# Moving the set-up of the TT weights and the transposes of W3 behind the first four layer-norm tiles

## The chip, the cores and the metric

The kernel runs on all 8 cores of one Trainium2 chip, each core taking one batch element. No core talks to another. The time is device microseconds of the slowest core.

## The reference

For each batch element x (4096 rows of 1024 numbers) the reference computes one block:

```python
xn = _layernorm(x, axis=-1)
Q = xn @ W1 + b1;  K = xn @ W2 + b2;  V = xn @ W3 + b3
attn = softmax(einsum('bse,bte->bst', Q, K) / 32)
a = einsum('bst,bte->bse', attn, V) @ W4 + b4
W_real = einsum('abcd,cefg->abefdg', G1_R, G2_R).reshape(512, 512)   # W_imag alike
out_real = xr @ W_real.T - xi @ W_imag.T + bias_real    # xr, xi: halves of xn
out_imag = xr @ W_imag.T + xi @ W_real.T + bias_imag
x = x + a + concatenate([out_real, out_imag], axis=-1)
```

## The kernel before

Every instruction is put on a list by `P.add(engine, ...)`. Each engine runs its own part of this list in exactly that order; a `waits=[...]` entry becomes a semaphore wait in front of the instruction, and everything later on the same engine stands behind it. DMAs issued by SP, ACT and POOL are entries of those engines' lists too.

The program has four stages.

1. **Prologue.** SP issues four loads of the small TT factors (G1 and G2, real and imaginary), then 16 loads of one column each of `b1` and `b2`, 8 of `b3`, and three bias rows. All 31 count on one semaphore; `PRO` is the wait for all of them. POOL issues the cast load of W3 into `Wproj` (line 211) and eight cast loads of W4 (line 215), and then makes the identity matrix `ident` and the ones (lines 218 to 223). DVE casts `b3` (line 226, `b3c`, waits for `PRO`) and permutes G2 (line 229, `g2perm`, waits for `PRO`). `emit_g(0)` does 8 rounds of a float32 matmul (line 236) and a DVE eviction (line 243) through the one PSUM tile `sp_a`, and ends with a 1 MB store to scratch by SP. Then PE transposes W3 in 32 pairs (lines 258 and 261, through `ptA` and `ptB`) and DVE evicts each pair into `W3T` (line 264). POOL's cast load of W2 (line 269, `LW2`) overwrites `Wproj`, so it waits for the last of these transposes.
2. **First tiles and group 0.** A layer-norm tile is 128 rows. `emit_ln_load` issues its 512 KB load on ACT into one of two slots of `xg`; the load of tile t waits until tile t-2 has been normalised. `emit_ln_stats` is four DVE instructions (lines 284 to 294), `emit_ln_apply` two ACT instructions, one DVE instruction (line 309) and one POOL instruction (line 313), and `emit_ln_tps` four pairs of PE transposes, each evicted by DVE (line 337) into `xnT`. Tiles 0 to 3 are done in pairs, ahead of the loop over groups. Group 0 then does both halves of its K projection (`emit_khalf`, line 357, which waits for W2 and for its tiles), and the prologue's tail: `emit_g(1)`, the product of W3 and W4 (line 402), the bias row, and 64 small read-backs of the scratch (line 449) that DVE turns into `Wq2` (line 455). Then come its V projection (line 379) and the next group's tiles. DVE reaches the evictions of tiles 4 and 5 only behind line 455.
3. **Groups 1 to 7** do K, V and the next group's tiles.
4. **Attention** over 32 row tiles, from about 460 us to the end, with the next rows' layer norm and Q projection in between.

The order of PE's list at the start of the program is: the matmuls of `emit_g(0)`, the transposes of W3, the transposes of tiles 0 to 3, K of group 0. DVE's list has `b3c` and `g2perm` first, then the matching evictions, then the statistics of tile 0. POOL's list has W3, W4, `ident`, W2, and then the normalisation of tile 0.

Of the kernel before, what the change touches and what calls it, by code (L numbers as in the profile page):

```python
# [9 lines left out]
ALU = mybir.AluOpType  # L10
# [62 lines left out]
def build_nc(T=4096):  # L73
# [11 lines left out]
    w2_d = nc.dram_tensor("W2", [D, D], F32, kind="ExternalInput").ap()  # L85
# [5 lines left out]
    g1r_d = nc.dram_tensor("G1R", [1, 32, 4, 32], F32, kind="ExternalInput").ap()  # L91
    g2r_d = nc.dram_tensor("G2R", [4, 16, 1, 16], F32, kind="ExternalInput").ap()
    g1i_d = nc.dram_tensor("G1I", [1, 32, 4, 32], F32, kind="ExternalInput").ap()
    g2i_d = nc.dram_tensor("G2I", [4, 16, 1, 16], F32, kind="ExternalInput").ap()
# [3 lines left out]
    scr_d = [nc.dram_tensor(f"scr{ri}", [1024, 256], F32).ap() for ri in range(2)]  # L98
# [7 lines left out]
    Wproj = E(nc.sbuf_tensor("Wproj", [128, 8, D], BF16))  # L106
# [8 lines left out]
    ident = E(nc.sbuf_tensor("ident", [128, 128], BF16))  # L115
# [3 lines left out]
    b3c = E(nc.sbuf_tensor("b3c", [128, 8], BF16))  # L119
    b3f = E(nc.sbuf_tensor("b3f", [128, 8], F32))  # L120
# [15 lines left out]
    ones1 = cbs[0:2, 1024:1152]  # L136
# [3 lines left out]
    if full:  # L140
        W3T = KT[:, :, 2048:3072]
    else:
        W3T = None
# [5 lines left out]
    else:  # L149
# [6 lines left out]
        W3T = W3T_t[:, :, :]  # L156
        pro_flat = pro_t[:, :]

    out2 = pro_flat[:, 0:4096].bitcast(F32).rearrange("p (q n) -> p q n", q=8)
    wqst = [pro_flat[:, 4096 + 1024 * k:4096 + 1024 * (k + 1)].bitcast(F32)  # L160
            for k in range(2)]
# [3 lines left out]
    g1p = pro_flat[0:4, 12288:16384].bitcast(F32).rearrange(  # L165
        "p (ri n) -> p ri n", ri=2)
    g2n = pro_flat[0:4, 16384:17408].bitcast(F32).rearrange(
        "p (ri n) -> p ri n", ri=2)
# [10 lines left out]

    semnames = ["q_sy", "q_t", "q_v", "q_s", "q_g",  # L180
                "d_pro", "d_wg", "d_xg0", "d_xg1", "d_xr", "d_out",
                "d_scw", "d_sra", "d_srb", "d_w10", "d_w11", "d_w12", "d_w13", "d_cbl", "d_wgB"]
    sems = {n: E(nc.semaphore(n)) for n in semnames}

    P = Prog()
# [3 lines left out]
    def proload(key, out_ap, in_ap):  # L189
        P.add("sync", lambda e, o=out_ap, i=in_ap: e.dma_start(o, i),  # L190
              mark=key, dma_sem="d_pro")

    proload(("Lg1r",), g1p[:, 0, :],
            bass.AP(g1r_d.tensor, 0, [[32, 4], [128, 32], [1, 32]]))
    proload(("Lg1i",), g1p[:, 1, :],
            bass.AP(g1i_d.tensor, 0, [[32, 4], [128, 32], [1, 32]]))
    proload(("Lg2r",), g2n[:, 0, :],
            bass.AP(g2r_d.tensor, 0, [[256, 4], [1, 256]]))
    proload(("Lg2i",), g2n[:, 1, :],
            bass.AP(g2i_d.tensor, 0, [[256, 4], [1, 256]]))  # L200
    for c in range(8):
        proload(("Lb1", c), b1s[:, c:c + 1], b1_d[c * 128:(c + 1) * 128].unsqueeze(1))
        proload(("Lb2", c), b2s[:, c:c + 1], b2_d[c * 128:(c + 1) * 128].unsqueeze(1))
    for c in range(8):
# [3 lines left out]
    proload(("Lbi",), cbrow[:, 512:1024], bi_d.unsqueeze(0))  # L208
    PRO = ("Lbi",)

    P.add("gpsimd", lambda e: e.dma_start(
        Wproj[:, :, :], w3_d.rearrange("(c p) n -> p c n", p=128)),
        mark=("LW3",), dma_sem="d_wg")
    for k4 in range(8):
        P.add("gpsimd", lambda e, k4=k4: e.dma_start(
            W4b[:, k4, :], w4_d[128 * k4:128 * (k4 + 1), :]),
            mark=("LW4", k4), dma_sem="d_wgB")
    P.add("gpsimd", lambda e: e.memset(ident[:, :], 0.0), mark=("id1",))
    P.add("gpsimd", lambda e: e.affine_select(
        out=ident[:, :], in_=ident[:, :], compare_op=ALU.not_equal, fill=1.0,  # L220
        base=0, pattern=[[-1, 128]], channel_multiplier=1),
        waits=[("id1",)], mark=("id2",))
    P.add("gpsimd", lambda e: e.memset(ones1, 1.0), mark=("ones",))
    WG0 = ("LW4", 7)

    P.add("vector", lambda e: e.tensor_copy(b3c[:, :], b3f[:, :]),
          waits=[PRO], mark=("Lb3c",))

    P.add("vector", lambda e: e.tensor_copy(
        g2p[:, :, :].rearrange("p ri (g e) -> p ri g e", g=16),  # L230
        g2n[:, :, :].rearrange("p ri (e g) -> p ri g e", e=16)),
        waits=[PRO], mark=("g2perm",))

    def emit_g(ri):
        for q in range(8):
            P.add("tensor", lambda e, ri=ri, q=q: e.matmul(
                sp_a[:, 0:256], g1p[:, ri, q * 128:(q + 1) * 128],
                g2p[:, ri, :], start=True, stop=True),
                waits=[PRO, ("g2perm",), free["sp_a"],
                       ("Gev", ri, q - 1) if q > 0 else  # L240
                       (("Gev", ri - 1, 7) if ri > 0 else None)],
                mark=("Gmm", ri, q))
            P.add("vector", lambda e, ri=ri, q=q: e.tensor_copy(
                out2[:, q, :], sp_a[:, 0:256]),
                waits=[("Gmm", ri, q)] + ([("scw", 0)] if ri == 1 else []),
                mark=("Gev", ri, q))
        P.add("sync", lambda e, ri=ri: e.dma_start(
            scr_d[ri].rearrange("(q p) n -> p q n", p=128), out2[:, :, :]),
            waits=[("Gev", ri, 7)],
            mark=("scw", ri), dma_sem="d_scw")  # L250
        free["sp_a"] = ("Gev", ri, 7)

    emit_g(0)
    for p2 in range(32):
        i, j2 = divmod(p2, 4)
        bank, bk = (ptA, "ptA") if p2 % 2 == 0 else (ptB, "ptB")
        j0 = 2 * j2
        P.add("tensor", lambda e, i=i, j0=j0, bank=bank: e.transpose(
            bank[:, 0, :], Wproj[:, i, j0 * 128:(j0 + 1) * 128], ident[:, :]),
            waits=[("LW3",), ("id2",), free[bk]], mark=None)  # L260
        P.add("tensor", lambda e, i=i, j0=j0, bank=bank: e.transpose(
            bank[:, 1, :], Wproj[:, i, (j0 + 1) * 128:(j0 + 2) * 128], ident[:, :]),
            mark=("w3tp", p2))
        P.add("vector", lambda e, i=i, j0=j0, bank=bank: e.tensor_copy(
            W3T[:, j0:j0 + 2, i * 128:(i + 1) * 128], bank[:, :, :]),
            waits=[("w3tp", p2)], mark=("w3te", p2))
        free[bk] = ("w3te", p2)

    P.add("gpsimd", lambda e: e.dma_start(
        Wproj[:, :, :], w2_d.rearrange("(c p) n -> p c n", p=128)),  # L270
        waits=[("w3tp", 31)], mark=("LW2",), dma_sem="d_wg")

    def emit_ln_load(gt):
        slot = gt % 2
# [49 lines left out]
    def emit_ln_tps(gt, phase, extra_tp):  # L324
        u = gt % 4
        slot = gt % 2
        for p4 in range(4):
            bank, bk = (ptA, "ptA") if p4 % 2 == 0 else (ptB, "ptB")
            c0 = 2 * p4
            xw = [("lnap", gt), free[bk]] + (list(extra_tp) if p4 == 0 else [])  # L330
            P.add("tensor", lambda e, c0=c0, slot=slot, bank=bank: e.transpose(  # L331
                bank[:, 0, :], xnn[:, slot, c0 * 128:(c0 + 1) * 128], ident[:, :]),
                waits=xw + [("id2",)], mark=None)
            P.add("tensor", lambda e, c0=c0, slot=slot, bank=bank: e.transpose(  # L334
                bank[:, 1, :], xnn[:, slot, (c0 + 1) * 128:(c0 + 2) * 128], ident[:, :]),
                mark=("xtp", gt, p4))
            P.add("vector", lambda e, u=u, c0=c0, bank=bank: e.tensor_copy(  # L337
                xnT[:, u, c0:c0 + 2, :], bank[:, :, :]),
                waits=[("xtp", gt, p4)], mark=("xte", gt, p4))
            free[bk] = ("xte", gt, p4)  # L340
        if phase == 2:
            P.add("gpsimd", lambda e, u=u: e.tensor_scalar_mul(
                ngxT[:, u, :],
                xnT[:, u, 4:8, :].rearrange("p c n -> p (c n)"), -1.0),
                waits=[("xte", gt, 2), ("xte", gt, 3)], mark=("ngx", gt))
# [112 lines left out]
        WQDONE = ("Wqcv", 1, 3)  # L458


    for u in range(2):
        emit_ln_load(u)
        emit_ln_stats(u)
# [8 lines left out]
        emit_ln_apply(u)  # L472
    for u in range(2, 4):
        emit_ln_tps(u, 1, [])
    for g in range(NGRP):
        nphase = 2 if g == NGRP - 1 else 1
        for u2 in range(2):
            emit_ln_load(4 * (g + 1) + u2)
            emit_ln_stats(4 * (g + 1) + u2)
        emit_khalf(g, 0)  # L480
        for u2 in range(2):
            emit_ln_apply(4 * (g + 1) + u2)
        if g == 0:
            emit_khalf(g, 1)
            emit_prologue_tail()
        emit_v(g, 0)
        emit_v(g, 1)
        for u2 in range(2):
            emit_ln_tps(4 * (g + 1) + u2, nphase,
                        [("Kmm", 0, g, 7), ("Vmm", g, u2, 1)])  # L490
        for u2 in range(2, 4):
            emit_ln_load(4 * (g + 1) + u2)
            emit_ln_stats(4 * (g + 1) + u2)
        if g > 0:
            emit_khalf(g, 1)
        for u2 in range(2, 4):
            emit_ln_apply(4 * (g + 1) + u2)
        emit_v(g, 2)
        emit_v(g, 3)
        for u2 in range(2, 4):  # L500
            emit_ln_tps(4 * (g + 1) + u2, nphase,
                        [("Kmm", 1, g, 7), ("Vmm", g, u2, 1)])
# [237 lines left out]
```

How the kernel before makes its waits and increments, by code:

```python
            def body(eng):  # L53
                seen = waited[engname]
                for e, fn, rw, mi in self.ops:
                    if e != engname:
                        continue
                    for semname, val in rw:
                        if seen.get(semname, -1) >= val:
                            continue
                        eng.wait_ge(sems[semname], val)
                        seen[semname] = val
                    ins = fn(eng)
                    if mi is not None:
                        semname, val, inc = mi
                        ins.then_inc(sems[semname], inc)
```

## Time and profile before

| | us |
|---|---|
| two timed runs | 1748.47 and 2000.08 |
| their median | 1874.27 |
| the profiled execution | 1748.35 |
| its span on the slowest core | 1746.6 |
| spans of the 8 cores | 1741.6 to 1746.6 |
| PE busy in the span | 1549.8 (89%) |
| DVE busy | 765.8 (44%) |
| ACT busy | 493.1 (28%) |
| POOL busy | 130.9 (7%) |

The span runs from the first to the last instruction of the slowest core, 1.75 us less than the time of that execution. A matmul's row is its time in the pipeline, so the busy time of PE overstates how near it is to its peak. Engines are PE (TensorE), PEld (its weight loads), DVE (VectorE), ACT (ScalarE), POOL (GpSimd) and SP (SyncE); SPq and ACTq are their queues issuing DMAs. PEclk is the granted clock of TensorE, 1.00 being 2.4 GHz.

### The profile page before, as it was taken

Reading aid. Unit: us, or ns where it says so; the run is one execution under the profiler, and the core shown is the slowest. Engines: PE = TensorE matmul, PEld = TensorE weight load, DVE = VectorE, ACT = ScalarE, POOL = GpSimd, SP = SyncE. Lnnn points to the kernel's source line nnn. Section 1 sums busy time; section 2 is a strip of 40 time slices with the busy share of each in tenths; the row PEclk is TensorE's granted clock in tenths of the full one; section 3 lists DMA queues with packets and bytes.
Section 4 is the critical chain, followed back from the end, with each engine's and each line's share of the span. In section 5 each row is a group of like instructions: output and inputs, shape, how many; then the busy total and the mean of one; then the engine's idle time right before and its main releaser. Section 6 shows DMA issues by size and latency. Waiting matters only on the chain.

```text
span 1746.6 us, 25605 instructions; the slowest of 8 cores (1741.6 to 1746.6 us)
## 1 busy us (share of the span) xinstructions
PE 1549.8 (89%) x8496; PEld 762.3 (44%) x8496; DVE 765.8 (44%) x1872; ACT 493.1 (28%) x865; POOL 130.9 (7%) x113
## 2 busy tenths in 40 slices
PE   0477299999899999999999999999999999999998
PEld 0143165655444444444444444444444444444443
DVE  0423233333355535553553555355535544553554
ACT  0010033333233323323223233233232232332322
POOL 1010011111100000000000000000000000000000
PEclk9989599999999999999999999999999999999999
DMA  7411421121411111101110111111111111110001
GB/s 122 93 52 32 43 71 60 63 73 49 136 45 38 37 37 37 45 29 42 45 51 35 41 45 37 37 37 38 36 37 49 49 36 37 49 37 25 25 25 37
DMA packets 69756, 83.49 MB, mean 48 GB/s; under 512 B 39923, under 2 KB 50171, under 8 KB 69630
## 3 DMA queue, kind: packets, MB, share of 16 engines
q1 hardware_dynamic: 57182, 42.02, 8.2%
q10 hardware_dynamic: 9216, 33.56, 5.8%
q0 software_dynamic: 3232, 6.29, 2.2%
q8 instruction: 72, 1.18, 0.3%
q14 instruction: 54, 0.44, 0.1%
HBM read 69.27 MB, written 18.87 MB: 50 GB/s over the span
## 4 chain that ended last, share of the span: by engine, by line
PE 85%; DVE 5%; SPq 4%; issue 3%; DMA 2%; ACT 0%; DVEq 0%; POOL 0%; ACTq 0%; POOLq 0%
PE po L558 13%; PE po L663 12%; PE po L659 12%; PE sp_a L558 6%; PE sp_b L558 6%; PE pf L588 3%; PE sp_a L357 3%; PE sp_b L357 3%; PE po L379 3%; PE pf L379 3%; PE sp_b L525 3%; PE sp_a L525 3%; PE ptA L630 2%; PE ptB L630 2%; DVE QXT L337 2%
## 5 line engine op out<-in xcount | busy, mean ns | idle before, releaser
L663 PE MATMUL po<-V,ETs 128*128 128x512 bf16 x1024 | 388.0, 379 | 0.0
L659 PE MATMUL po<-V,ETs 128*128 128x512 bf16 x1024 | 388.0, 379 | 0.0
L558 PE MATMUL po<-KT,QXT 128*128 128x512 bf16 x1024 | 231.5, 379 | 0.0
L614 ACT ACTIVATE Et<-Ssb,ngm 128x512 bf16<-128x512 f32 x256 | 181.2, 719 | 165.5 <-PE ptB L630 139.0
L618 DVE TENSOR_REDUCE r<-Et 128x1 f32<-128x512 bf16 x256 | 173.7, 679 | 31.1 <-ACT Et L614 31.1
L313 POOL TENSOR_SCALAR xnn<-xg,rstd,nmr 128x1024 bf16<-128x1024 f32 x64 | 76.2, 1196 | 1231.8 <-DVE nmr L309 1217.1
L558 PEld LDWEIGHTS po<-KT,QXT 128*128 128x128 bf16 x1024 | 100.2, 98 | 120.9
L563 DVE TENSOR_REDUCE mx<-po 128x1 f32<-128x512 f32 x128 | 88.6, 692 | 129.6 <-PE po L558 129.6
L663 PEld LDWEIGHTS po<-V,ETs 128*128 128x128 bf16 x1024 | 100.1, 98 | 94.3
L659 PEld LDWEIGHTS po<-V,ETs 128*128 128x128 bf16 x1024 | 100.0, 98 | 94.4
L571 ACT ACTIVATE Ssb<-sp_a 128x512 f32<-128x512 f32 x64 | 38.2, 597 | 341.5 <-DVE mx L563 188.0
L642 DVE COPY ETs<-ptA 128x256 bf16<-128x256 bf16 x256 | 73.5, 287 | 134.4 <-PE ptB L630 98.2
L558 PE MATMUL sp_a<-KT,QXT 128*128 128x512 bf16 x512 | 120.9, 379 | 7.7 <-ACT QXT L533 7.7
L558 PE MATMUL sp_b<-KT,QXT 128*128 128x512 bf16 x512 | 120.9, 379 | 0.0
L571 ACT ACTIVATE Ssb<-po 128x512 f32<-128x512 f32 x128 | 76.4, 597 | 142.0 <-DVE mx L563 142.0
L331 PE MATMUL ptA<-ident,xnn 128*128 128x128 bf16 x128 | 28.3, 221 | 95.8 <-DVE QXT L337 77.0
L337 DVE COPY QXT<-ptA 128x256 bf16<-128x256 bf16 x128 | 37.4, 292 | 156.2 <-PE ptB L334 96.9
L563 DVE TENSOR_REDUCE mx<-sp_a 128x1 f32<-128x512 f32 x64 | 44.1, 689 | 135.7 <-PE sp_a L558 135.7
L630 PE MATMUL ptA<-ident,Et 128*128 128x128 bf16 x512 | 70.4, 219 | 24.9 <-DVE ETs L642 15.2
L692 DVE SCALAR_TENSOR_TENSOR xr<-po,rrv,xr 128x1024 f32<-128x1024 f32 x32 | 41.1, 1284 | 92.1 <-PE po L663 92.1
L558 PEld LDWEIGHTS sp_a<-KT,QXT 128*128 128x128 bf16 x512 | 49.5, 98 | 70.0 <-issue 11.4
L630 PEld LDWEIGHTS ptA<-ident,Et 128*128 128x128 bf16 x512 | 41.5, 97 | 82.7 <-issue 50.6
(95 smaller groups left out, 1809.9 us busy)
## 6 DMA issues: line engine op xcount, KB each, us to landing
xg<-x ACTq DMA_DIRECT2D x64, 512.0 KB, 3.6
xr<-x SPq DMA_DIRECT2D x32, 512.0 KB, 3.5
out<-xr SPq DMA_DIRECT2D x32, 512.0 KB, 2.6
Wproj<-W POOLq DMA_DIRECT2D x2, 2048.0 KB, 21.1
Ssb<-W SPq DMA_DIRECT2D x8, 512.0 KB, 8.0
KT<-W POOLq DMA_DIRECT2D x8, 256.0 KB, 25.9
scr<-V SPq DMA_DIRECT2D x2, 1024.0 KB, 4.5
V<-scr SPq DMA_DIRECT2D x64, 32.0 KB, 2.5
```

The costliest lines, as they stand in the source:

```text
L313: P.add("gpsimd", lambda e, s=s: e.tensor_scalar(xnn[:, s, :], xg[:, s, :], rstd[:, s, 0:1], nmr[:, s, 0:1], ALU.mult, ALU.add), waits=[(" ...
L357: e.matmul(spv[:, off:off + 256], Wproj[:, k, c * 128:(c + 1) * 128], xnT[:, 2 * half:2 * half + 2, k, :], start=(k == 0), stop=(k == 7)),
L379: P.add("tensor", lambda e, u=u, h=h, k=k, pv=pv: e.matmul(pv[:, h * 512:(h + 1) * 512], xnT[:, u, k, :], W3p[:, k, h * 512:(h + 1) * 512] ...
L525: P.add("tensor", lambda e, r=r, k=k, spv=spv: e.matmul(spv[:, :], Wproj[:, r, k * 128:(k + 1) * 128], xnT[:, :, k, :], start=(k == 0), st ...
L558: P.add("tensor", lambda e, tb=tb, c=c, si=si, spv=spv: e.matmul(spv, QT[:, c, si * 128:(si + 1) * 128], KT[:, c, tb * 512:(tb + 1) * 512] ...
L563: P.add("vector", lambda e, tb=tb, spv=spv: e.reduce_max(mx8[:, tb:tb + 1], spv, axis=AX.X), waits=[("Smm", i, tb)], mark=("Smx", i, tb))
L571: P.add("scalar", lambda e, tb=tb, spv=spv: e.activation(Ssb[:, tb * 512:(tb + 1) * 512], spv, AF.Identity), waits=scw_, mark=("Scp", i, tb))
L614: P.add("scalar", lambda e, tb=tb: e.activation(Et[:, tb % 2, :], Ssb[:, tb * 512:(tb + 1) * 512], AF.Exp, bias=ngm[:, 0:1], scale=SCALE), ...
L618: P.add("vector", lambda e, tb=tb: e.reduce_sum(r8[:, tb:tb + 1], Et[:, tb % 2, :], axis=AX.X), waits=[("exp", i, tb)] + ([("rr", i - 1)] ...
L630: e.transpose(bank[:, qq, :], Et[:, tb % 2, q * 128:(q + 1) * 128], ident[:, :]),
L659: P.add("tensor", lambda e, tb=tb, q=q, tj=tj: e.matmul(po[:, 0:512], ETs[:, tb % 2, q, :], V0[:, tj, 0:512], start=(tj == 0), stop=(tj == ...
L663: P.add("tensor", lambda e, tb=tb, q=q, tj=tj: e.matmul(po[:, 512:1024], ETs[:, tb % 2, q, :], V0[:, tj, 512:1024], start=(tj == 0), stop= ...
```

## The change

Five things are changed, and no instruction is added to or taken from the program:

- The four loads of G1 and G2 count on a semaphore of their own, and `GLD` is the wait for them. `PRO` is now the wait for the other 27 loads.
- `ident` and the ones are made by POOL ahead of its loads of W3 and W4.
- `b3c`, with its wait for `PRO`, stands directly ahead of the loop that starts layer-norm tile 0.
- `g2perm` and `emit_g(0)`, which now wait for `GLD` in place of `PRO`, and the 32 pairs of transposes of W3 with their evictions stand behind the layer norm and the transposes of tiles 0 to 3.
- The load of W2 stands behind these, and so behind the normalisation of tiles 0 to 3 in POOL's list.

```diff
+    P.add("gpsimd", lambda e: e.memset(ident[:, :], 0.0), mark=("id1",))
     P.add("gpsimd", lambda e: e.dma_start(
         Wproj[:, :, :], w3_d.rearrange("(c p) n -> p c n", p=128)),
         mark=("LW3",), dma_sem="d_wg")
...
-    P.add("vector", lambda e: e.tensor_copy(b3c[:, :], b3f[:, :]),
-          waits=[PRO], mark=("Lb3c",))
...
+    P.add("vector", lambda e: e.tensor_copy(b3c[:, :], b3f[:, :]),
+          waits=[PRO], mark=("Lb3c",))
+
     for u in range(2):
         emit_ln_load(u)
         emit_ln_stats(u)
...
     for u in range(2, 4):
         emit_ln_tps(u, 1, [])
+    P.add("vector", lambda e: e.tensor_copy(
+        g2p[:, :, :].rearrange("p ri (g e) -> p ri g e", g=16),
+        g2n[:, :, :].rearrange("p ri (e g) -> p ri g e", e=16)),
+        waits=[GLD], mark=("g2perm",))
...
+                waits=[GLD, ("g2perm",), free["sp_a"],
...
+    emit_g(0)
...
+    P.add("gpsimd", lambda e: e.dma_start(
+        Wproj[:, :, :], w2_d.rearrange("(c p) n -> p c n", p=128)),
+        waits=[("w3tp", 31)], mark=("LW2",), dma_sem="d_wg")
+
     for g in range(NGRP):
```

## Rows read from the trace of the kernel before

**Rows 1.** Spans and mean granted TensorE clock, two of eight cores
```profile
core 2: 1746.6 us, clock 0.980
...
core 4: 1746.6 us, clock 0.978
```

**Rows 2.** Stages: length, busy PE PEld DVE ACT POOL, clock, DMA share, GB/s
```profile
0.00:34.60 34.60, 0.00 (x0) 0.00 (x0) 0.00 (x0) 0.00 (x0) 6.18 (x16) 1.00 0.98 153
...
64.90:88.50 23.60, 4.45 (x32) 2.36 (x33) 11.08 (x34) 2.91 (x9) 5.66 (x5) 1.00 0.75 161
...
160.10:203.20 43.10, 0.00 (x0) 0.00 (x0) 3.32 (x8) 0.50 (x1) 0.00 (x0) 0.53 0.59 73
```

**Rows 3.** Chain that ended last, 60 to 92 us: start, length, what
```profile
71.61 9.80 DMA xg<-x
```

**Rows 4.** Timeline of the first 50 us: start, length, engine, line, operation
```profile
1.56 1.06 POOL L211 DMA_DIRECT2D Wproj<-W  x1 [0.87 <-POOLq L79]
...
6.81 0.31 POOL L218 MEMSET ident<- 128x128 bf16 x1
...
7.56 0.19 POOL L223 MEMSET cbs<- 2x128 bf16 x1
...
29.87 0.25 SPq L190 DMA_DIRECT2D V<-bim  x1
...
34.63 0.17 DVE L226 CAST b3c<-b3f 128x8 bf16<-128x8 f32 x1 [34.63 <-DMA V<-bim]
```

**Rows 5.** Timeline from 64 to 89 us, the same columns
```profile
64.70 0.69 DVE L284 BATCH_NORM_STATS2 bn<-xg 128x6 f32<-128x512 f32 x1
...
64.94 0.92 POOL L269 DMA_DIRECT2D Wproj<-W  x1 [57.19 <-PE ptB L261]
...
70.42 1.52 ACTq L278 DMA_DIRECT2D xg<-x  x2
...
74.04 0.29 DVE L337 COPY QXT<-ptB 128x256 bf16<-128x256 bf16 x1
...
81.50 0.69 DVE L284 BATCH_NORM_STATS2 bn<-xg 128x6 f32<-128x512 f32 x1 [0.89 <-DMA xg<-x]
...
88.54 1.91 PE L357 MATMUL sp_a<-QXT,Wproj 128*128 128x256 bf16 x8
...
88.85 0.29 DVE L337 COPY QXT<-ptB 128x256 bf16<-128x256 bf16 x1
```

**Rows 6.** Loads of tile xg from 0 to 110 us, issue to landing
```profile
DMA to landing us min/median/max: 3.5/4.9/9.8
```

**Rows 7.** DMA, 65 to 82 us: packets, MB, share; an issue's landing
```profile
q0 software_dynamic: 1040, 2.10, 73.2%
...
q10 hardware_dynamic: 288, 1.05, 17.8%
...
Wproj<-W POOLq DMA_DIRECT2D x1, 2048.0 KB, 17.0
```

**Rows 8.** Core 2 by line: min/median/max ns, first and last start; W2's landing
```profile
L226 DVE CAST b3c<-b3f x1: 172/172/172, 39.1 to 39.1; 128x8 bf16<-128x8 f32 x1
...
L269 POOL DMA_DIRECT2D Wproj<-W x1: 914/914/914, 69.4 to 69.4; - x1
...
L357 PE MATMUL sp_a<-QXT,Wproj x64: 269/272/418, 94.1 to 108.8; 128*128 128x256 bf16 x64
...
Wproj<-W POOLq DMA_DIRECT2D x1, 2048.0 KB, 19.6
```

**Rows 9.** Timeline: V projection of tiles 2 and 3 of group 0
```profile
206.12 5.91 PE L379 MATMUL po<-Ssb,QXT 128*128 128x512 bf16 x16
...
211.86 3.62 PE L379 MATMUL pf<-Ssb,QXT 128*128 128x512 bf16 x16
```

**Rows 10.** Line 455, cores 2 and 4: duration ns, first and last start
```profile
L455 DVE CAST Wq<-V x8: 426/427/428, 174.0 to 204.0; 128x512 bf16<-128x512 f32 x8
...
L455 DVE CAST Wq<-V x8: 426/427/428, 169.4 to 202.9; 128x512 bf16<-128x512 f32 x8
```

More of the change, by code:

```diff
@@ L181, in build_nc @@
                 "d_pro", "d_wg", "d_xg0", "d_xg1", "d_xr", "d_out",
-                "d_scw", "d_sra", "d_srb", "d_w10", "d_w11", "d_w12", "d_w13", "d_cbl", "d_wgB"]
+                "d_scw", "d_sra", "d_srb", "d_w10", "d_w11", "d_w12", "d_w13", "d_cbl", "d_wgB", "d_gld"]
     sems = {n: E(nc.semaphore(n)) for n in semnames}
@@ L191, in proload, with gload @@
               mark=key, dma_sem="d_pro")
[L193 to L200, printed above, removed]
+    def gload(key, out_ap, in_ap):
+        P.add("sync", lambda e, o=out_ap, i=in_ap: e.dma_start(o, i),
+              mark=key, dma_sem="d_gld")
+    gload(("Lg1r",), g1p[:, 0, :],
+          bass.AP(g1r_d.tensor, 0, [[32, 4], [128, 32], [1, 32]]))
+    gload(("Lg1i",), g1p[:, 1, :],
+          bass.AP(g1i_d.tensor, 0, [[32, 4], [128, 32], [1, 32]]))
+    gload(("Lg2r",), g2n[:, 0, :],
+          bass.AP(g2r_d.tensor, 0, [[256, 4], [1, 256]]))
+    gload(("Lg2i",), g2n[:, 1, :],
+          bass.AP(g2i_d.tensor, 0, [[256, 4], [1, 256]]))
+    GLD = ("Lg2i",)
     for c in range(8):
@@ L209, in build_nc @@
     PRO = ("Lbi",)
+    P.add("gpsimd", lambda e: e.memset(ident[:, :], 0.0), mark=("id1",))
+    P.add("gpsimd", lambda e: e.affine_select(
+        out=ident[:, :], in_=ident[:, :], compare_op=ALU.not_equal, fill=1.0,
+        base=0, pattern=[[-1, 128]], channel_multiplier=1),
+        waits=[("id1",)], mark=("id2",))
+    P.add("gpsimd", lambda e: e.memset(ones1, 1.0), mark=("ones",))
     P.add("gpsimd", lambda e: e.dma_start(
@@ L217, in build_nc @@
             mark=("LW4", k4), dma_sem="d_wgB")
[L218 to L223, printed above, removed]
-    WG0 = ("LW4", 7)
-    P.add("vector", lambda e: e.tensor_copy(b3c[:, :], b3f[:, :]),
-          waits=[PRO], mark=("Lb3c",))
@@ L229, in build_nc @@
[L229 to L267, printed above, removed]
@@ L269, in build_nc @@
-    P.add("gpsimd", lambda e: e.dma_start(
-        Wproj[:, :, :], w2_d.rearrange("(c p) n -> p c n", p=128)),
-        waits=[("w3tp", 31)], mark=("LW2",), dma_sem="d_wg")
+    WG0 = ("LW4", 7)
     def emit_ln_load(gt):
@@ L474, in build_nc, with emit_g @@
         emit_ln_tps(u, 1, [])
+    P.add("vector", lambda e: e.tensor_copy(
+        g2p[:, :, :].rearrange("p ri (g e) -> p ri g e", g=16),
+        g2n[:, :, :].rearrange("p ri (e g) -> p ri g e", e=16)),
+        waits=[GLD], mark=("g2perm",))
+    def emit_g(ri):
+        for q in range(8):
+            P.add("tensor", lambda e, ri=ri, q=q: e.matmul(
+                sp_a[:, 0:256], g1p[:, ri, q * 128:(q + 1) * 128],
+                g2p[:, ri, :], start=True, stop=True),
+                waits=[GLD, ("g2perm",), free["sp_a"],
+                       ("Gev", ri, q - 1) if q > 0 else
+                       (("Gev", ri - 1, 7) if ri > 0 else None)],
+                mark=("Gmm", ri, q))
+            P.add("vector", lambda e, ri=ri, q=q: e.tensor_copy(
+                out2[:, q, :], sp_a[:, 0:256]),
+                waits=[("Gmm", ri, q)] + ([("scw", 0)] if ri == 1 else []),
+                mark=("Gev", ri, q))
+        P.add("sync", lambda e, ri=ri: e.dma_start(
+            scr_d[ri].rearrange("(q p) n -> p q n", p=128), out2[:, :, :]),
+            waits=[("Gev", ri, 7)],
+            mark=("scw", ri), dma_sem="d_scw")
+        free["sp_a"] = ("Gev", ri, 7)
+    emit_g(0)
+    for p2 in range(32):
+        i, j2 = divmod(p2, 4)
+        bank, bk = (ptA, "ptA") if p2 % 2 == 0 else (ptB, "ptB")
+        j0 = 2 * j2
+        P.add("tensor", lambda e, i=i, j0=j0, bank=bank: e.transpose(
+            bank[:, 0, :], Wproj[:, i, j0 * 128:(j0 + 1) * 128], ident[:, :]),
+            waits=[("LW3",), ("id2",), free[bk]], mark=None)
+        P.add("tensor", lambda e, i=i, j0=j0, bank=bank: e.transpose(
+            bank[:, 1, :], Wproj[:, i, (j0 + 1) * 128:(j0 + 2) * 128], ident[:, :]),
+            mark=("w3tp", p2))
+        P.add("vector", lambda e, i=i, j0=j0, bank=bank: e.tensor_copy(
+            W3T[:, j0:j0 + 2, i * 128:(i + 1) * 128], bank[:, :, :]),
+            waits=[("w3tp", p2)], mark=("w3te", p2))
+        free[bk] = ("w3te", p2)
+    P.add("gpsimd", lambda e: e.dma_start(
+        Wproj[:, :, :], w2_d.rearrange("(c p) n -> p c n", p=128)),
+        waits=[("w3tp", 31)], mark=("LW2",), dma_sem="d_wg")
     for g in range(NGRP):
```

## The prediction

> **What bounds the kernel now.** I read the spans of the cores first: cores 2 and 4 tie as the slowest with 1746.6 us [rows 1], so the page's core, core 4, is followed here and core 2 beside it. The sum is made against the profiled execution, 1748.35 us, which is 1.75 us above its span and 0.12 us below the timed run of 1748.47 us. The other timed run, 2000.08 us, is a disturbed one that pulls the median to 1874.27 us, so the forecast is for an undisturbed run.
>
> The change touches only the first 88.5 us, so I cut the span into stages. Until 34.60 us PE and DVE are idle while the DMA engines are 0.98 busy; from 64.90 to 88.50 us PE works 4.45 of 23.60 us; from 160.10 to 203.20 us it does nothing [rows 2]. The head is a serial chain. POOL issues W3 at 1.56 us, SP's last bias load is issued at 29.87 us, and its landing releases `b3c` on DVE at 34.63 us [rows 4]. From there the chain goes through the TT product and the transposes of W3 to POOL's issue of W2 at 64.94 us [rows 5]. Until then no layer norm has been done; statistics of tile 0 start at 64.70 us, and the last eviction of tile 3 is the row at 88.85 us, just after K's first matmuls at 88.54 us [rows 5]. So **the 23.6 us of layer norm run under W2's load**, which takes 17.0 us from issue to landing [rows 7], to 81.94 us. What ends last ahead of K is not W2 but the layer norm, held by a load of x: the chain shows 9.80 us of it from 71.61 us [rows 3].
>
> **The change part by part.**
>
> *The waits.* `GLD` frees the TT product from 27 bias loads, but it is not DVE's first entry. `b3c` is, and it still waits for all 27. Statistics of tile 0 stand behind it, and `g2perm` behind those. DVE therefore starts at the same 34.63 us [rows 4]. Gain of the new semaphore: 0.
>
> *POOL's memsets.* The stretch from the first memset at 6.81 to the end of the last at 7.75 us [rows 4] is 0.94 us, and W3 and W4 are issued that much later. The DMA engines are 0.98 busy until 34.60 us [rows 2], so if the bias loads end with the weights, `PRO` comes 0.94 us later. Against this, more of the bias loads may be issued ahead of the weights. SP's 31 load issues are over at 30.12 us, 0.97 us each, while the last takes 0.25 us [rows 4]; two that slip ahead save at most 1.5 us. I take 0 and keep -1.5 to +0.9.
>
> *Layer norm, tiles 0 and 1.* The same instructions, started behind `b3c`. From 64.70 to the end of the row at 74.04 us, 74.33 us, it is 9.63 us [rows 5].
>
> *Layer norm, tiles 2 and 3.* Their loads are issued 5.72 us after the statistics of tile 0 begin (70.42 less 64.70), now at 40.5 us, and meet idle DMA engines instead of W2. They land after 3.5 us, the shortest xg row, or 4.9 us, the median [rows 6]: 44.0 to 45.4 us, against 44.4 us when tile 1 is through. I take 3.5 and keep +1.0 for the other end. The block is 2.0 us (statistics of tile 2, as tile 0 before tile 1) and then, from tile 3's statistics at 81.50 to 89.14 us, 7.64 us [rows 5]: 9.64 us. This is faster than before, where it waited for x, but it hid W2 then and hides nothing now.
>
> *TT product, transposes of W3.* From `b3c` at 34.63 to W2's issue at 64.94 us is 30.31 us [rows 4, 5], one DVE or PE step after the other, and it is moved whole. W2's issue comes at 34.63 + 9.63 + 9.64 + 30.31 = 84.2 us, 19.3 us later. On POOL it now stands behind four normalisations that are over by 50 us, which costs nothing. On SP only the store to scratch moves; nothing reads it until group 0's tail. On PE, K waits behind it all.
>
> *W2's load.* Before it took 17.0 us with tiles 2 and 3 on the same DMA engines. In the 17 us from 65 to 82 us the queue of x took 17.8% [rows 7], 3.0 us, so W2 without it takes 14.0 us. Bounds: W2's own queue took 73.2% of the 17 us, 12.4 us, the least possible; 17.0 us if the memory and not the engines set its pace. K can start at 84.2 + 14.0 = 98.2 us where it started at 88.54: **+9.7 us**, within +8.1 and +12.7.
>
> The Trainium skill ("DMA: Bandwidth & Descriptors", section "Issuing engines are not separate DMA queues") says that DMAs issued by scalar, sync or gpsimd run on the same 16 engines and interleave. By it the 3.0 us are to be taken off; a reader who thinks of the queues as separate would leave them in, and come out at +12.7 us.
>
> *PE's clock.* K's first eight matmuls took 1.91 us [rows 5], and core 2's single ones range from 418 ns to 269 ns [rows 8]: it starts at 1.2 GHz and rises to 2.4. Transposes ran just before it. Now PE is idle for some 14 us first. The nearest case is V after the idle stretch of 43 us: 5.91 us for the first 16 matmuls against 3.62 us for the next 16 [rows 9], a loss of 2.3 us, against at least 1.2 us that K loses now (its first eight matmuls, 418 less 269 ns each [rows 8]). So +0 to +1.1 us; I take +0.5.
>
> The Trainium skill ("TensorE: Matmul & The Clock Gate", section "What's actually happening") has it that half rate is the default and activity lifts it. By that rule the idle stretch costs something here, and by the rule alone it cannot cost more than one more slow start.
>
> *Everything behind K's start* keeps its order: the tail's products, the read-backs, groups 1 to 7, attention. None of it waits for anything with a time of its own, so it shifts as a block.
>
> *Core 2.* `PRO` lands at 39.1 us, W2 is issued at 69.4, takes 19.6 us, and K starts at 94.1 us [rows 8]. By the same steps 39.1 + 19.3 + 30.3 + (19.6 - 3.0) = 105.3 us, +11.2 us. The two slowest cores give +9.7 and +11.2; the middle is 10.5, and with the clock's 0.5 **+11.0 us**. 1748.35 + 11.0 = 1759.3, say **1759 us**.
>
> **The rivals.**
>
> 1. *Layer norm under the bias loads (faster).* If DVE took up tile 0 when x has landed, some 5 us in, all four tiles would be done by 34 us. Then W2 goes out at 64.9 us as before, lands alone after 14.0 us, and K starts at 79 us: 9.6 us earlier, **1739 us**. For it: DVE has nothing to do for 34.6 us. Against it: `b3c` heads DVE's list and waits for `Lbi`. It decides if `PRO` lands before 25 us, 9.7 us sooner. Chance 0.04.
> 2. *Part of the shift is absorbed.* Core 2 starts K 5.6 us behind core 4, but starts its last `Wq2` cast only 1.1 us behind it, 204.0 against 202.9 us [rows 10], and both spans are 1746.6 us. If the read-backs run at a pace that the cores share, some 4.5 us of the shift go there. Against it: all cores are shifted alike, so there is no one to overtake. 1759 less 5 is **1754 us**. Chance 0.13.
> 3. *W2 gains nothing from being alone.* All eight cores load W2 at about the same time. It takes 17.0 us on core 4 and 19.6 on core 2 as before, x lands late (+1.0), W3 delays `PRO` (+0.9): core 2 then shifts by 11.2 + 3.0 + 1.0 + 0.9 + 0.5, 16.6 us, **1765 us**. Chance 0.13.
> 4. *The forecast*, +8 to +14 us, 1756 to 1762 us. Chance 0.70.
>
> **How the numbers follow.** The predicted time is that of case 4, 1759 us. The range takes in cases 2 and 3 and 2 to 4 us around them for the spread of the cores: 1750 to 1768 us; case 1 is left out. A measurement of this kernel can tell about 2%, 35 us. No case reaches that: case 1 is -0.5%, case 3 +1.0%. So within 2% has 0.95, slower 0.04 and faster 0.01, these two for what I have not seen. The sign is clearer than the size: slower by any amount 0.95.
>
> **What would show it.** In the profile after, `b3c` starts at about 34.6 us (core 4) and the next DVE row is line 284's; xg's loads of tiles 2 and 3 land in under 5 us; W2 is issued near 84 us and lands 14 us later; K begins near 98 us with PE idle since 84 us; the stretch from K's start to the end is as before within 3 us. If the statistics of tile 0 start well before 30 us, or W2 goes out before 75 us, the forecast is wrong at its first step. If W2 takes 17 us or more, it is wrong in its price. If K starts at 98 us and the end moves by less than 5 us, case 2 is right.

## The result

| | before | after |
|---|---|---|
| median of the timed runs (10 and 11) | 1749.44 us | 1756.69 us |
| the profiled execution | 1748.35 us | 1755.22 us |
| its span, slowest core | 1746.6 us | 1753.6 us |
| spans of the 8 cores | 1741.6 to 1746.6 us | 1747.3 to 1753.6 us |

The changed kernel is slower: ratio 1.0042, 95% interval 1.0031 to 1.0052. On 1749.4 us that is +7.3 us, between +5.4 and +9.1. The forecast was +11.0 us, to 1759 us. The sign and the mechanism at the head are right; the size is too large, and by a term that was not in the sum at all. In one execution of the changed kernel, 1797.61 us, four cores ran at a granted clock of 0.95 to 0.96 where the others had 0.98; the ratios, here and in every experiment below, leave out such disturbed executions, and the one of 2000.08 us before.

Core 4 of the changed kernel, stage by stage (the columns are those of [rows 2]): the layer norm of tiles 0 to 3, then TT product and transposes of W3, then the wait for W2.

```profile
35.70:54.80 19.10, 4.69 (x32) 2.34 (x32) 11.40 (x36) 2.90 (x9) 4.74 (x4) 1.00 0.29 97
54.80:84.90 30.10, 18.87 (x80) 8.44 (x80) 12.44 (x44) 0.00 (x0) 0.00 (x0) 1.00 0.13 44
84.90:100.40 15.50, 0.00 (x1) 0.03 (x1) 3.21 (x8) 0.00 (x0) 0.94 (x1) 1.00 0.85 135
```

The clock of 1.00 in these rows, and in the rows of the kernel before up to 88.5 us, is no measurement: the trace of core 4 has its first record of the clock at 104.7 us (before: at 91.3 us), and K's first matmuls, ahead of it, take 417 ns each, the lower of the two levels (1.2 GHz), against 269 to 273 ns behind it.

The same stretch in the timeline (start, length, engine, line, operation; the bracket tells the idle time before and what ended it). Lines 419, 242, 436, 476 and 315 are lines 226, 284, 229, 269 and 357 of the kernel before:

```profile
35.69 0.17 DVE L419 CAST b3c<-b3f 128x8 bf16<-128x8 f32 x1 [35.69 <-DMA V<-bim]
35.80 0.69 DVE L242 BATCH_NORM_STATS2 bn<-xg 128x6 f32<-128x512 f32 x1
...
55.10 0.57 DVE L436 COPY V<-V 4x512 f32<-4x512 f32 x1
...
84.92 0.94 POOL L476 DMA_DIRECT2D Wproj<-W  x1 [32.55 <-PE ptB L468]
...
100.40 1.86 PE L315 MATMUL sp_a<-QXT,Wproj 128*128 128x256 bf16 x8 [16.04 <-DMA Wproj<-W]
```

`b3c` still heads DVE's list and still waits for the last bias load, as in [rows 4]. Statistics of tile 0 follow it at once, 19.3 us of layer norm stand ahead of `g2perm`, and K is released by W2's landing, where it was released by the last tile. W2 is alone on the DMA engines. Between 84.5 and 101 us the DMA view has no queue of x beside it, where [rows 7] has 17.8%:

```profile
q0 software_dynamic: 1040, 2.10, 79.8%
issues: line engine op xcount, KB each, median us to landing
Wproj<-W POOLq DMA_DIRECT2D x1, 2048.0 KB, 15.3
```

A single core is a poor witness here, since the landing of the bias loads wanders between 32.5 and 41.0 us from core to core and from run to run (core 2: 39.1 us before, 34.5 us after). So I took the same marks from all eight cores of each profiled execution. Means over the cores, in us from the span's start. The columns from `order only` on are the experiments below (the changed order without the new semaphore, the semaphore without the order, one wait more, `b3c` moved, and `b3c` moved with the TT product first):

```text
                               before  after  order  sem.   one    b3c    TT
                                              only   only   wait   late   first
b3c starts                       37.1   37.1   37.2   37.1   37.7   89.4   75.0
statistics of tile 0             67.2   37.2   37.3   66.8   67.4    5.9   38.8
W2 issued                        67.4   86.4   86.4   67.0   67.7   62.2   39.1
K starts                         91.9  102.4  101.9   91.3   92.7   78.3   64.4
product of W3 and W4 starts     120.8  132.1  131.3  120.9  122.2  108.1   94.0
last cast into Wq2              203.3  213.8  213.9  202.6  205.0  190.0  176.0
Q of the first group            459.3  469.9  469.8  459.1  461.3  445.7  430.8
attention, first to last tile  1224.8 1219.9 1224.8 1219.8 1219.8 1219.8 1219.8
mean span                      1744.1 1749.7 1754.3 1738.7 1741.1 1725.0 1710.4
```

The first two columns hold the puzzle. K starts 10.5 us later; the product of W3 and W4 starts 11.3 us later, and the last cast and the Q projection again 10.5 us. Then the attention stage, whose instructions are the same in both kernels, is 4.9 us shorter. It is so on every core: 1224.8 us on all eight before, 1219.8 to 1220.0 us after. The mean span grows by the rest, 5.6 us; the slowest core's span grew by 7.0 us in these two executions.

### The profile page after: what moved, and what is told of

It reads as the page before. It is cut to its first block, busy times and chain, and to the rows that moved or that the text cites. A ratio compares the mean times of both kernels' runs of the same rounds, so it can differ in the third digit from the quotient of the medians.

```text
span 1753.6 us, 25600 instructions; the slowest of 8 cores (1747.3 to 1753.6 us)
## 1 busy us (share of the span) xinstructions
PE 1551.1 (88%) x8496; PEld 763.7 (44%) x8496; DVE 765.6 (44%) x1872; ACT 492.9 (28%) x865; POOL 130.9 (7%) x113
## 4 chain that ended last, share of the span: by engine, by line
PE 87%; DVE 4%; SPq 4%; issue 2%; DMA 2%; ACT 0%; DVEq 0%; POOL 0%; ACTq 0%; POOLq 0%
PE po L563 13%; PE po L668 13%; PE po L664 13%; PE sp_a L563 6%; PE sp_b L563 6%; PE pf L593 3%; PE sp_a L315 3%; PE sp_b L315 3%; PE sp_a L530 3%; PE sp_b L530 3%; PE po L337 3%; PE pf L337 3%; PE ptA L635 2%; DVE QXT L295 2%; PE ptB L635 2%
## 5 line engine op out<-in xcount | busy, mean ns | idle before, releaser
L568 DVE TENSOR_REDUCE mx<-po 128x1 f32<-128x512 f32 x128 | 88.5, 692 | 132.5 <-PE po L563 132.5
L635 PE MATMUL ptA<-ident,Et 128*128 128x128 bf16 x512 | 70.4, 219 | 23.5 <-DVE ETs L647 13.8
L315 PE MATMUL sp_a<-QXT,Wproj 128*128 128x256 bf16 x512 | 68.7, 279 | 18.0 <-DMA Wproj<-W 17.6
L563 PEld LDWEIGHTS sp_a<-KT,QXT 128*128 128x128 bf16 x512 | 49.6, 98 | 70.0 <-issue 11.4
```

Of the source, the lines that this page charges most:

```text
L315: e.matmul(spv[:, off:off + 256], Wproj[:, k, c * 128:(c + 1) * 128], xnT[:, 2 * half:2 * half + 2, k, :], start=(k == 0), stop=(k == 7)),
L563: P.add("tensor", lambda e, tb=tb, c=c, si=si, spv=spv: e.matmul(spv, QT[:, c, si * 128:(si + 1) * 128], KT[:, c, tb * 512:(tb + 1) * 512] ...
L568: P.add("vector", lambda e, tb=tb, spv=spv: e.reduce_max(mx8[:, tb:tb + 1], spv, axis=AX.X), waits=[("Smm", i, tb)], mark=("Smx", i, tb))
L635: e.transpose(bank[:, qq, :], Et[:, tb % 2, q * 128:(q + 1) * 128], ident[:, :]),
```

## Where attention gave 4.9 us back

The combining instruction that closes a row tile (line 692, 697 in the changed kernel) is a good clock. Before, core 4:

```profile
515.94 1.28 DVE L692 SCALAR_TENSOR_TENSOR xr<-po,rrv,xr 128x1024 f32<-128x1024 f32 x1 [2.89 <-PE po L663]
...
552.48 1.28 DVE L692 SCALAR_TENSOR_TENSOR xr<-po,rrv,xr 128x1024 f32<-128x1024 f32 x1 [2.88 <-PE po L663]
...
589.04 1.28 DVE L692 SCALAR_TENSOR_TENSOR xr<-po,rrv,xr 128x1024 f32<-128x1024 f32 x1 [2.88 <-PE po L663]
```

After, core 4:

```profile
521.84 1.28 DVE L697 SCALAR_TENSOR_TENSOR xr<-po,rrv,xr 128x1024 f32<-128x1024 f32 x1 [2.89 <-PE po L668]
...
558.03 1.28 DVE L697 SCALAR_TENSOR_TENSOR xr<-po,rrv,xr 128x1024 f32<-128x1024 f32 x1 [2.88 <-PE po L668]
...
594.23 1.28 DVE L697 SCALAR_TENSOR_TENSOR xr<-po,rrv,xr 128x1024 f32<-128x1024 f32 x1 [2.88 <-PE po L668]
```

The intervals are 36.54 and 36.56 us before, 36.19 and 36.20 us after. Before, in each of the first seven groups of four tiles, the first two intervals are 36.55 us and the third 36.20 us; after, all three are 36.20 us. That is 14 x 0.35 = 4.9 us, the whole difference.

Inside such an interval the two kernels run alike up to one DVE instruction, the first eviction of a layer-norm transpose. In the kernel before:

```profile
581.10 0.22 PE L334 MATMUL ptB<-ident,xnn 128*128 128x128 bf16 x1
581.66 0.29 DVE L337 COPY QXT<-ptA 128x256 bf16<-128x256 bf16 x1 [1.81 <-PE ptB L334]
581.87 0.28 DVE L337 COPY QXT<-ptB 128x256 bf16<-128x256 bf16 x1
```

It starts 0.56 us after PE's fourth transpose starts. Its semaphore wait had ended at 581.27 us, and DVE has no record in the 0.4 us between. An instruction elsewhere starts 0.04 us behind its wait (in the changed kernel one wait ends at 488.904 us and its instruction starts at 488.948 us), so 0.35 us of the 0.40 are lost, which is what the interval has too much. The list of all such late starts was made by numbering the entries of DVE's list from 0, waits included, in order of time, and looking for an instruction that starts over 0.2 us after both its own wait and the work before it had ended:

```text
kernel before, core 4              changed kernel, core 4
entry   start us  line  delay us   entry   line
  827    483.40    563    0.40     827     a wait, at 488.9 us; nothing late behind it
  955    536.55    287    0.40     955     a wait; nothing late behind it
 1083    581.66    337    0.40     ...
 1211    643.80    563    0.40     no late start from 460 us to the end
 1339    696.96    287    0.40
 1467    742.09    337    0.41
 ... to entry 3643, 128 apart, 23 in all
```

From 460 us on, and up to entry 3643, every 128th entry comes 0.4 us late. Ahead of the attention stage too, entries 59, 315, 571 and 699 are late behind their waits, by 0.26 to 0.46 us, and these numbers lie on the same grid (59 plus a multiple of 128). A group of attention has 384 entries, three times 128, so the same three places are hit in each group. Before, all three are an instruction just behind its wait, so the delay starts when the wait has ended, and it is on the path twice in a group. The changed kernel's list has one entry more, 3827 against 3826: `g2perm` waits for `GLD`, where it found `PRO` already awaited by `b3c` and needed no wait. From there on each late place in the attention stage falls on a wait, which would be standing idle or behind a running instruction anyway. Outside it the grid still shows: entry 187 of the changed kernel is an instruction behind its wait, and it starts 0.41 us late (at 119.7 us). PE's and POOL's lists change their lengths as well, by 4 and 2 entries less, so they have to be kept apart from DVE's entry. This is a theory (A) that makes sharp predictions. Its rival (B) is that attention is shorter for another reason, such as the time at which it starts or the loads of x ahead of it.

## The experiments

**One entry more, nothing else.** The kernel before, with a wait for the identity, which has long been made:

```diff
         g2n[:, :, :].rearrange("p ri (e g) -> p ri g e", e=16)),
-        waits=[PRO], mark=("g2perm",))
+        waits=[PRO, ("id2",)], mark=("g2perm",))
```

> The kernel before, with one satisfied semaphore wait more in DVE's list: g2perm also waits for the identity, which is made at 7.6 us and needed at 34.6 us. Theory A (every 128th entry of DVE's list starts 0.4 us late, and it shows only where that entry is the instruction behind a wait): the late starts fall on waits and vanish, the two intervals of 36.55 us per group of attention become 36.2 us, 14 x 0.35 = 4.9 us less: ratio to the kernel before 0.9972. Theory B (the attention stage of the changed kernel is shorter for another reason, such as the time at which it starts or the earlier loads of x): no change, ratio 1.000.

Measured: median 1744.69 us against 1748.8 us, ratio 0.9986, interval 0.9967 to 1.0005. The interval is wide, since one run of the twelve took 1761.7 us, and by time alone it does not settle the matter (the other nine in the ratio average 1744.7 us, which would be 0.9977; leaving one out after the fact proves nothing). The trace does. Attention takes 1219.8 to 1219.9 us on all eight cores, 5.0 us less than before, and DVE has no late start behind a wait in it:

```profile
515.74 1.28 DVE L692 SCALAR_TENSOR_TENSOR xr<-po,rrv,xr 128x1024 f32<-128x1024 f32 x1 [2.89 <-PE po L663]
...
551.93 1.28 DVE L692 SCALAR_TENSOR_TENSOR xr<-po,rrv,xr 128x1024 f32<-128x1024 f32 x1 [2.88 <-PE po L663]
...
580.54 0.22 PE L334 MATMUL ptB<-ident,xnn 128*128 128x128 bf16 x1
...
580.75 0.29 DVE L337 COPY QXT<-ptA 128x256 bf16<-128x256 bf16 x1 [1.46 <-PE ptB L334]
...
588.13 1.28 DVE L692 SCALAR_TENSOR_TENSOR xr<-po,rrv,xr 128x1024 f32<-128x1024 f32 x1 [2.88 <-PE po L663]
```

Intervals of 36.19 and 36.20 us, and the eviction 0.21 us behind the transpose's start instead of 0.56. A wait that waits for nothing makes attention 5 us shorter, in a kernel whose lists on PE and POOL are those of the kernel before, and whose attention starts 2 us later and not 10: theory A.

**The order of the change, without the entry.** The changed kernel with the four loads back on the old semaphore:

```diff
-              mark=key, dma_sem="d_gld")
+              mark=key, dma_sem="d_pro")
...
-    GLD = ("Lg2i",)
+    GLD = PRO
```

> The changed kernel with its four loads of G1 and G2 counted on the old semaphore again, so that g2perm needs no wait of its own and DVE's list has one entry less. Order of all instructions as in the changed kernel. Theory A: K starts at 102.4 us on average as in the changed kernel, the attention stage is 4.9 us longer than there, and the time is 1749.4 + 10.6 = 1760 us, ratio to the kernel before 1.0060. Theory B: as the changed kernel, ratio 1.0042.

Measured: median 1760.37 us, ratio 1.0067, interval 1.0055 to 1.0079, which is +11.7 us (9.6 to 13.8). The late starts are back at entries 827, 955, 1083 and on, and with them the long intervals, 36.54 and 36.54 us:

```profile
526.56 1.28 DVE L697 SCALAR_TENSOR_TENSOR xr<-po,rrv,xr 128x1024 f32<-128x1024 f32 x1 [2.89 <-PE po L668]
...
563.10 1.28 DVE L697 SCALAR_TENSOR_TENSOR xr<-po,rrv,xr 128x1024 f32<-128x1024 f32 x1 [2.88 <-PE po L668]
...
592.27 0.29 DVE L295 COPY QXT<-ptA 128x256 bf16<-128x256 bf16 x1 [1.81 <-PE ptB L292]
...
599.64 1.28 DVE L697 SCALAR_TENSOR_TENSOR xr<-po,rrv,xr 128x1024 f32<-128x1024 f32 x1 [2.88 <-PE po L668]
```

K starts 10.0 us later than before on average, and attention takes 1224.8 us on all eight cores: nothing is given back. PE's and POOL's lists have the lengths of the changed kernel here, so these don't shorten attention. This is the shift that the forecast worked out, and its time too.

**The semaphore alone.** The kernel before with the loads of G1 and G2 on their own semaphore, in the old order (of the edit, the wait of `g2perm`; the four loads and the waits of `emit_g` change with it):

```diff
-        waits=[PRO], mark=("g2perm",))
+        waits=[GLD], mark=("g2perm",))
```

> The kernel before with only the new semaphore for the loads of G1 and G2: same order of instructions, g2perm waits for it behind b3c. Theory A: the head is unchanged (W2 issued at 67.5 us on average), the attention stage 4.9 us shorter, ratio to the kernel before 0.9972. Theory B: ratio 1.000.

Measured: median 1744.09 us, ratio 0.9975, interval 0.9966 to 0.9984, -4.4 us (2.8 to 5.9). The head is as before, W2 issued at 67.0 us, and attention is 1219.8 us. The two halves of the change add up: +11.7 - 4.4 = +7.3 us, the measured change.

**Two entries more.**

```diff
-        waits=[PRO], mark=("g2perm",))
+        waits=[PRO, ("id1",), ("id2",)], mark=("g2perm",))
```

> The kernel before with two satisfied waits more in DVE's list. Theory A: the late starts are back, now on the instruction one wait-and-instruction pair ahead of where the kernel before has them. Whether they lie on the path depends on that place: between 0 and 4.9 us less than before, ratio 0.9972 to 1.000, and the trace shows the 0.4 us delays again, 128 entries apart. Theory B: 1.000 and no delays of this kind tied to the count.

Measured: median 1745.1 us, ratio 0.998, interval 0.9971 to 0.9988. Attention takes 1220.5 us. Here the place counts and not only whether there are one or two entries more: of the three late places of a group, that of line 563 is again the instruction behind a wait (0.40 us late, and on the path neither here nor before). The second now falls on the statistics of line 284, which starts with no delay that can be seen, behind an eviction that keeps DVE busy. The third falls on an eviction of the exponentials (line 642), which starts 0.40 us behind its wait but only 0.17 us behind the eviction ahead of it. Only 0.09 us per group shows in an interval (36.29, 36.20, 36.20). My expectation allowed anything from 0.9972 to 1.000, so this run bounds the effect rather than testing it. Over all eight kernels the count decides: 3826 entries in DVE's list (the kernel before and order only) go with 1224.8 us of attention, 3827 (the changed kernel, one wait, the semaphore alone and the two kernels below) with 1219.8 to 1219.9 us on average, 3828 with 1220.5 us.

**The bias wait taken from the head of DVE's list.** The changed kernel, with `b3c` moved:

```diff
-    P.add("vector", lambda e: e.tensor_copy(b3c[:, :], b3f[:, :]),
-          waits=[PRO], mark=("Lb3c",))
-
     for u in range(2):
         emit_ln_load(u)
...
             emit_khalf(g, 1)
+            P.add("vector", lambda e: e.tensor_copy(b3c[:, :], b3f[:, :]),
+                  waits=[PRO], mark=("Lb3c",))
             emit_prologue_tail()
```

> The changed kernel with b3c, the one entry that waits for the 27 bias loads, moved from the head of DVE's list to just ahead of the prologue's tail. Theory A (b3c alone keeps DVE idle until 37 us): statistics of tile 0 start at some 6 us, all four tiles are done by about 32 us, W2 is issued near 62 us and K starts near 78 us, 24.8 us earlier than in the changed kernel and 14.3 us earlier than before. With the attention stage as in the changed kernel, 1749.4 - 14.3 - 4.9 = 1730 us, ratio 0.989. Theory B (DVE would be held anyway, by the landing of x among the weight loads): statistics of tile 0 start only when the weights have landed, above 30 us, and the time stays near 1757 us.

Measured: 1730.3 to 1731.5 us in three executions, ratio 0.9894, interval 0.986 to 0.9928. Timeline of core 4:

```profile
6.10 0.69 DVE L242 BATCH_NORM_STATS2 bn<-xg 128x6 f32<-128x512 f32 x1 [6.10 <-DMA xg<-x]
...
22.88 0.69 DVE L242 BATCH_NORM_STATS2 bn<-xg 128x6 f32<-128x512 f32 x1 [7.00 <-DMA xg<-x]
...
63.37 0.95 POOL L473 DMA_DIRECT2D Wproj<-W  x1 [32.46 <-PE ptB L465]
...
80.25 1.87 PE L315 MATMUL sp_a<-QXT,Wproj 128*128 128x256 bf16 x8 [17.44 <-DMA Wproj<-W]
```

One cast of 0.17 us held everything behind it for 31 us: statistics of tile 0 start at 5.9 us instead of 37.2 us on average (core 4: 6.1 and 35.8 us), and K at 78.3 us. This is rival 1 of the forecast, which put K at 79 us. Part of the early start is lost again: the loads of tiles 2 and 3 now run beside those of W3 and W4, and DVE waits 7.00 us for tile 2.

**The old order, with the bias wait out of the way.** The semaphore of its own and `b3c` moved as above, but TT product, transposes and W2 ahead of the layer norm.

> The order of the kernel before (TT product, transposes of W3, load of W2, then the layer norm), with the semaphore of its own for G1 and G2 and with b3c moved to just ahead of the prologue's tail. Theory A (what costs is the layer norm standing ahead of W2's issue, and the bias wait at the head of DVE's list): the TT product starts at some 6 us, the transposes of W3 are held by W3's landing at about 21 us, W2 is issued near 36 us, the layer norm lies under its load again, and K starts near 61 us: 31 us earlier than before and 17 us earlier than with the layer norm first. 1749.4 - 31 - 4.9 = 1713 us, ratio 0.980. Theory B (the order doesn't matter once the bias wait is gone): 1730 us, as the kernel with the layer norm first.

Measured: median 1716.5 us, ratio 0.9815, interval 0.9792 to 0.9838. It beats both kernels, by 32 us and by 40 us. The 32 us are 27.5 us by which K starts earlier (64.4 against 91.9 us) and the 5.0 us of attention. Core 4:

```profile
8.77 0.58 DVE L231 COPY V<-V 4x512 f32<-4x512 f32 x1 [8.77 <-DMA V<-G2I]
...
38.62 0.68 DVE L286 BATCH_NORM_STATS2 bn<-xg 128x6 f32<-128x512 f32 x1
38.87 0.92 POOL L271 DMA_DIRECT2D Wproj<-W  x1 [31.09 <-PE ptB L263]
...
54.01 0.69 DVE L286 BATCH_NORM_STATS2 bn<-xg 128x6 f32<-128x512 f32 x1 [5.76 <-DMA xg<-x]
...
64.80 1.48 PE L359 MATMUL sp_a<-QXT,Wproj 128*128 128x256 bf16 x6
```

K starts at 64.4 us on average, 13.9 us earlier than with the layer norm first: the layer norm lies under W2's load again. I had put K at 61 us. The small factors land at 8.8 us and not at 6, and the load of x for tile 2 comes late beside W2: DVE waits 5.76 us for it (the row at 54.01 us).

## Why the forecast was right in sign and too large

- *Start at `PRO`, gain of the early wait 0.* Right: 37.1 us on average in both (over a scatter of 5 us between cores), and line 242 is the next DVE row behind `b3c`. The late `b3c` shows the other side of it.
- *POOL's memsets, 0.* Right as far as can be seen, by the same 37.1 us. W3 is issued 0.47 us later and not 0.94 us (2.03 against 1.56 us on core 4), and a cost of that size would drown in the scatter of the landings.
- *Layer norm 9.63 + 9.64 us, then 30.31 us to W2's issue.* Right: W2 is issued 49.3 us after `b3c` on average (86.4 less 37.1), 49.6 was forecast. The loads of tiles 2 and 3 held nothing up on core 4: no wait for x stands ahead of their statistics.
- *W2 alone, 3.0 us less.* Right on average: W2 took 18.7 us on the average core before and 15.8 us after. Single cores scatter, from 13.9 to 17.1 us after; core 4 gained only 1.7 us (17.0 to 15.3), core 2 gained 5.7 us (19.6 to 13.9). By the rule of the Trainium skill cited in the forecast, W2's landing had to gain what the load of x no longer takes; the trace agrees, with 2.9 us on average. Rival 3, no gain, falls.
- *K +9.7 and +11.2 us, clock +0.5.* The average over the eight cores is +10.5, the middle that was taken. On the two cores of the forecast K moved by +11.9 us (core 4) and +3.6 us (core 2), for their bias loads and W2 landed otherwise; that two cores gave the mean of eight is in part luck. The clock's term is right: counted from the traces, 19.5 of K's first 128 matmuls took 417 ns on average, against 14.6 before, and the 128 took 16.7 us against 16.3. From K's start to the product of W3 and W4 it is 29.7 us instead of 28.9, 0.8 more in all, but nothing of this 0.8 is left at the last cast into `Wq2`.
- *Everything behind K shifts as a block.* **This step failed.** It holds as far as the Q projection, +10.5 us. Attention then took 4.9 us less. The forecast's own sign, that the stretch from K's start to the end stays within 3 us, came out against it: 1647.3 us on average after, 1652.2 us before. Rival 2 had 5 us given back, the right amount, but in the read-backs of the scratch. Those took 40.6 us after and 41.3 us before, from the last cast ahead of them to the last into `Wq2`, so only 0.7 us went there. Its amount was right for a wrong reason.
- *Gain of the new semaphore, 0.* **The same failure seen from its cause.** I asked only what the new wait would free, and not what the entry itself does to the list. Alone it is worth -4.4 us, and attention is 5.0 us shorter by it.

With that term the sum is 11.0 - 4.9 = +6.1 us, against +7.3 us (5.4 to 9.1). That the measured 1756.7 us lies as near to the forecast 1759 as it does owes nothing to a term for the list: there was none. Without the entry the measured shift was +11.7 us against the forecast +11.0.

What is not settled in full is why every 128th entry is late. The traces do record a fetch of instructions. On the page of the kernel before, two DMA queues are of this kind:

```profile
q8 instruction: 72, 1.18, 0.3%
q14 instruction: 54, 0.44, 0.1%
```

The packets of q14 in the span hold 8192 bytes each, and on core 4 one of them starts 0.65 to 1.11 us behind each of the 23 late starts listed above. In the changed kernel, at the same 23 numbers of DVE's list, one starts 0.77 to 1.32 us behind the start of the instruction ahead of the wait, in 16 of the 23 cases before that wait has ended. This fits a list that comes in blocks of 128 entries, of 64 bytes each by these numbers, with another block asked for at each late place. The Trainium skill ("Runtime: NRT & Kernel Launch", section "Instruction fetch mechanics") describes a list that is fetched in blocks of 256 instructions, with the crossing of a block mostly hidden. The packets of q8 have 16384 bytes, 256 times 64, but DVE's spacing here is 128 entries, and a crossing costs 0.4 us where the entry follows a wait and lies on the path. What DVE does in the 0.4 us no trace shows: the packet comes behind the late start, so that it was waited for is not shown. What is shown is the spacing, the packet at each place, and that one harmless entry removes the cost and taking it out brings it back.

## What to carry to other kernels

An engine's list runs in order, so freeing a wait is worth nothing while another entry ahead of it waits for the same thing: look for the first entry that waits, and move that. Work that hides a load must stay behind the load's issue; here moving 19.3 us of it ahead cost 10.5 us, and the old order with the 0.17 us cast moved gained 32 us, 5 of them by the entry. In a long unrolled kernel, count entries before you explain a few us: two versions that differ by one entry in an engine's list can differ by 5 us in a stage that neither touched, so compare such versions by intervals within a stage and not by total time.

## What I had not expected of the hardware

Every 128th entry of DVE's list starts 0.4 us late, 23 times in the attention stage of the kernel before (483 to 1664 us), and whether this is paid depends on what stands there: 4.9 us of 1749 in one alignment, 0.6 us in another (1220.5 us of attention), nothing visible in a third. ACT's list shows late starts of the same kind, of 0.32 us, at entries 315, 699, 827 and 1083 among others, on the same grid as DVE's, in both kernels alike.

The landing of the last bias load varies from 32.5 to 41.0 us between cores and executions, with SP's load issues in the same order, while attention repeats to 0.2 us over the eight cores of a run. A head that ends with a landing should be compared by its mean over the cores.
